# Layer 2's k-sums packed to 64 columns and moved ahead of the clip, its second reciprocal ahead of an addition, and 39 blocks in layer 3

## What is computed

```python
def _chunk_abc(q, k, v, s):
    z = jax.lax.cumlogsumexp(s, axis=2)
    g = jnp.exp(jnp.concatenate([z[:, :, :1], z[:, :, :-1]], axis=2) - z)
    p = jnp.exp(s - z)
    ...
    def step_k(hk, x):
        hk = hk * g_t[:, :, None, :] + k_t[..., None] * p_t[:, :, None, :]
        return (hk, jnp.einsum('bhk,bhkm->bhm', q_t, hk))
    ...
    pvT = jax.nn.softmax(okT, axis=-1)
    def step_v(hv, x):
        hv = hv * g_t[..., None] + p_t[..., None] * v_t[:, :, None, :]
        return (hv, jnp.einsum('bhm,bhmv->bhv', pv_t, hv))
...
s = jnp.clip(to_heads(hidden_states @ Ws, M), CLAMP_MIN, CLAMP_MAX)
o = o * jax.lax.rsqrt(jnp.mean(jnp.square(o), axis=-1, keepdims=True) + EPS) * g_norm_weight
o = o * (g * jax.nn.sigmoid(g))
return o.reshape(b, t, VALUE_DIM) @ Wo
```

```python
top_logits, top_idx = jax.lax.top_k(logits, K)
...
for e in range(E):
    h = jax.nn.silu(x @ w0[e]) * (x @ w1[e])
    out = out + cw[:, e:e + 1] * (h @ wo[e])
```

## Time and profile before

| | |
|---|---|
| median of 3 runs | 2171.97 us (2171.43 to 2173.82) |
| the profiled execution, its own time | 2193.66 us |
| its span | 2192.1 us |
| mean granted TensorE clock | 0.92 of full |
| TensorE (PE) busy | 1875.1 us, 86% |
| VectorE (DVE) busy | 1399.3 us, 64% |
| ScalarE (ACT) busy | 680.2 us, 31% |
| GpSimd (POOL) busy | 565.3 us, 26% |

### The profile page before, as it was taken

One profiled execution on the slowest core, in us unless ns is written; L12 is line 12 of the kernel. 1 busy time (PEld: TensorE's weight loads), 2 busy tenths in 40 slices (PEclk: granted clock), 3 DMA queues, 4 the chain that ended last, 5 costly groups with the idle time before them and its releaser, 6 DMA issues. The chain is left out here.

```text
span 2192.1 us, 35525 instructions
## 1 busy us (share of the span) xinstructions
PE 1875.1 (86%) x13312; PEld 1444.0 (66%) x13312; DVE 1399.3 (64%) x3037; ACT 680.2 (31%) x1205; POOL 565.3 (26%) x552
## 2 busy tenths in 40 slices
PE   5943479971999999999999997989988988989995
PEld 2341357760888888888888886455566876756663
DVE  4476355548777777777777776476656777533334
ACT  2231334441333232323333332235534323222221
POOL 0234615550021212212121211532332103401111
PEclk9975579995999999999999998999998996999998
DMA  9329224426000000000000100000001006111114
GB/s 325 122 74 296 80 82 152 151 97 199 1 1 22 1 23 12 12 23 1 23 1 23 32 1 1 1 1 2 2 1 51 27 1 240 69 37 47 47 47 134
DMA packets 100639, 134.97 MB, mean 62 GB/s; under 512 B 11616, under 2 KB 73980, under 8 KB 99968
## 3 DMA queue, kind: packets, MB, share of 16 engines
q1 hardware_dynamic: 89344, 102.16, 14.7%
q0 software_dynamic: 11136, 30.62, 3.9%
HBM read 81.94 MB, written 50.81 MB: 61 GB/s over the span
## 5 line engine op out<-in xcount | busy, mean ns | idle before, releaser
L1114 POOL TENSOR_TENSOR a_rstd<-a_ms,consts 128x8 f32<-128x8 f32 x32 | 52.4, 1638 | 590.0 <-DVE a_ms L1466 590.0
L110 PE MATMUL a_ring<-a_w_hi,l_xnT_hi 128*128 128x256 f32 x512 | 157.3, 307 | 0.0
L110 PE MATMUL a_ring<-a_w_hi,l_xnT_lo 128*128 128x256 f32 x512 | 144.2, 282 | 0.0
L110 PE MATMUL a_ring<-a_w_lo,l_xnT_hi 128*128 128x256 f32 x512 | 144.0, 281 | 0.0
L2456 POOL DMA_INDIRECT l_slots_in<-xn,f_row_of x96 | 98.5, 1026 | 97.6 <-DVE f_row_of L2750 36.6
L2983 POOL DMA_INDIRECT l_pairs_out<-f_yb,f_to_row x96 | 96.2, 1002 | 101.6 <-ACT f_yb L2958 64.2
L1219 PE MATMUL a_pab<-a_w_o,a_oT 128*128 128x256 f32 x512 | 119.2, 387 | 1.2 <-ACT a_oT L1358 1.2
L1421 DVE RECIPROCAL a_rT<-a_rT 128x256 f32<-128x256 f32 x64 | 111.4, 1742 | 0.0
L1219 PEld LDWEIGHTS a_pab<-a_w_o,a_oT 128*128 128x128 f32 x512 | 100.2, 201 | 11.6 <-ACT a_oT L1358 1.6
L1704 PE MATMUL b_ring<-b_keys,b_qm 32*128 32x128 f32 (+2 forms) x896 | 91.2, 339 | 14.9 <-DVE b_nm L1917 9.4
L1465 DVE TENSOR_REDUCE a_ms<-a_on 128x8 f32<-128x1024 f32 x32 | 39.0, 1220 | 100.9 <-ACT a_on L1378 100.9
(11 more groups left out here) (495 smaller groups left out, 5069.6 us busy)
## 6 DMA issues: line engine op xcount, KB each, us to landing
l_slots_in<-l_zeros SPq DMA_DIRECT2D x4, 3120.0 KB, 22.3
f_xb<-l_slots_in SPq DMA_DIRECT2D x11, 1040.0 KB
f_gate_up_w<-l_pairs_out SPq DMA_DIRECT2D x16, 512.0 KB, 8.7
l_slots_in<-l_zeros SPq DMA_DIRECT2D x4, 1300.0 KB, 15.4
f_xb<-l_slots_in SPq DMA_DIRECT2D x40, 130.0 KB, 2.0
f_down_w<-L_ffn_w_down_dram SPq DMA_DIRECT2D x1, 4096.0 KB
f_gate_w<-L_ffn_w_dram SPq DMA_DIRECT2D x2, 2048.0 KB, 11.1
f_up_w<-L_ffn_w_dram SPq DMA_DIRECT2D x2, 2048.0 KB, 19.8
```

The costliest lines, as they stand in the source:

```text
L110: ins = pe.matmul(out, a, b, start=start and k == 0, stop=stop and k == 2, **kw)
L1114: pool.tensor_tensor(rstd[:], ms[:], core.consts[:, C_HALF:C_HALF + 8], ALU.pow).then_inc(s["rstd_ready"], 1)
```

## The change

Four edits. The k-sums are kept as 64 columns a chunk for both heads: `chunk_sums` writes both heads' sums to the same columns and different partitions, `prefix_k` makes three instructions on 128 partitions in place of six on 64, `ok` makes two products of half the rows and half the columns for each chunk in place of one, and the memset with its semaphore goes. `prefix_k` stands ahead of the clip of s. The second half of the reciprocals stands ahead of the addition to x. Layer 3 has 39 blocks, and its slots are cleared by three transfers of 13 blocks, a row (1,040 bytes) at a time; layer 1's clearing is the same as before.

```diff
-    hk, hv = st.sb("hk", [P, 3, P]), st.sb("hv", [P, 3, DV])
+    hk, hv = st.sb("hk", [P, 3, DK]), st.sb("hv", [P, 3, DV])
...
-            pool.memset(hk[:], 0.0).then_inc(s["zeros"], 1)
...
-            pe.wait_ge(s["zeros"], 1)
...
-                        ins = pe.matmul(pc[m, c * P + DK * h:c * P + DK * h + DK], k_tok[:, k % 2, c, m],
-                                        e_tok[:, k % 2, c, m], start=True, stop=True)
+                        ins = pe.matmul(pc[m, c * DK:(c + 1) * DK], k_tok[:, k % 2, c, m], e_tok[:, k % 2, c, m],
+                                        start=True, stop=True)
...
-                pe.wait_ge(s["hk_step"], 6 * (u + 1))
+                pe.wait_ge(s["hk_step"], 3 * (u + 1))
                 for c in range(1, NCH):
-                    pe.matmul(pc[:, c * P:(c + 1) * P], hk[:, c - 1, :], qT[:, k % 2, c * P:(c + 1) * P],
-                              start=(c == 1), stop=False, skip_group_check=True)
+                    for h in range(2):
+                        m = slice(DK * h, DK * h + DK)
+                        pe.matmul(pc[m, c * P:(c + 1) * P], hk[m, c - 1, :], qT[m, k % 2, c * P:(c + 1) * P],
+                                  start=(c == 1), stop=False, skip_group_check=True)
...
-            dve.wait_ge(s["zeros"], 1)
...
-                do = Steps(dve, s["hk_step"], 6 * u, 6)
+                do = Steps(dve, s["hk_step"], 3 * u, 3)
                 for c in range(3):
-                    for h in range(2):
-                        r = slice(DK * h, DK * h + DK)
-                        new = pc[r, c * P + DK * h:c * P + DK * h + DK]
-                        if c:
-                            do(dve.tensor_tensor(hk[r, c, r], new, hk[r, c - 1, r], ALU.add))
-                        else:
-                            do(dve.tensor_copy(hk[r, c, r], new))
+                    new = pc[:, c * DK:(c + 1) * DK]
+                    if c:
+                        do(dve.tensor_tensor(hk[:, c, :], new, hk[:, c - 1, :], ALU.add))
+                    else:
+                        do(dve.tensor_copy(hk[:, c, :], new))
...
                 prefix_v(u)
+                prefix_k(u)
                 if not last:
                     project_s(n, kn)
-                prefix_k(u)
...
+                if not last:
+                    project_r(n, kn, 1)
                 if not first:
                     emit(u - 1, (k - 1) % PER)
-                if not last:
-                    project_r(n, kn, 1)
...
-        self.blocks = self.K * TILES + self.E
+        self.blocks = self.K * TILES + self.E - self.FEWER
...
 class Slots3(Slots):
+    FEWER, CLEARS = 1, 3
+
+    def clearings(self, zeros):
+        n = self.blocks // self.CLEARS
+        for k in range(self.CLEARS):
+            yield (self.xs[k * n * P:(k + 1) * n * P, :].rearrange("(n q) d -> q n d", q=P),
+                   zeros[:, 0:ROW].unsqueeze(1).to_broadcast([P, n, ROW]))
...
-                sp.wait_ge(stored[k], 16 * (NB // RING))
+                sp.wait_ge(stored[k], 16 * len(range(k, NB, RING)))
```

More of the change, by code:

```diff
@@ L1032, in layer2_abc @@
              "c_ready r_ready v_copied tanh_ready gate_ready k_turned e_turned k_tok_ready e_tok_ready "
-             "scores_ready sm_ready hk_sums hk_step ok_ready lgT_ready lg_turned hv_sums hv_step zeros logit_step ex_ready "
+             "scores_ready sm_ready hk_sums hk_step ok_ready lgT_ready lg_turned hv_sums hv_step logit_step ex_ready "
              "den_step wt_ready w_turned wT_ready am_sums am_ready ov_ready sq_ready ms_step rstd_ready "
@@ L2428, in __init__ @@
         self.router_in, self.ROUTER = st.sem("router_in"), 16 * (1 + (spec.router_bias is not None))
-        self.CLEARS = 4
     def clear(self, sp, zeros):
[L2432 to L2435, removed]
+        for rows, zero in self.clearings(zeros):
+            sp.dma_start(rows, zero).then_inc(self.cleared, 16)
     def place_pairs(self, st):
@@ L2478 @@
 class Slots1(Slots):
+    FEWER, CLEARS = 0, 4
+    def clearings(self, zeros):
+        n = self.blocks // (2 * self.CLEARS)
+        for k in range(self.CLEARS):
+            yield (self.xs[k * n * 2 * P:(k + 1) * n * 2 * P, :].rearrange("(n q i) d -> q n (i d)", q=P, i=2),
+                   zeros[:].unsqueeze(1).to_broadcast([P, n, 2 * ROW]))
     def place(self, st):
```

## The result

| | before | after |
|---|---|---|
| median of the timed runs | 2171.81 us (2171.43 to 2173.82, 4 runs) | 2144.4 us (2140.79 to 2147.38, 4 runs) |
| the profiled execution, its own time | 2193.66 us | 2147.38 us |
| its span | 2192.1 us | 2145.6 us |

The ratio is 0.9871, with a 95% interval from 0.9854 to 0.9888: 27.4 us less, a faster kernel. Forecast were 2138 us and a range from 2127 to 2157.

The account below looks back on a forecast made before the run. TensorE's queue was taken to bound layer 2's linear attention: 18.6 + 10.2 - 1.6 + 0.75 = 28.0 us, with the block 33.8, subtracted from the median 2171.97 to give 2138 us; range 2127 to 2157.

Parts of the forecast that it names:

- The k wait: Layer 2's linear attention: TensorE no longer waits for VectorE's last k-sum; 0.62 us in each of units 1 to 30, 18.6 us.
- the shape: `ok` on TensorE: twelve quarter-product records and one more change of shape cost 0.05 us more in all 32 units, 1.6 us.
- The `wT` wait: TensorE's products of `weights` no longer wait for `wT`, the reciprocal filling VectorE's idle 0.97 us; 0.33 us in 31 units, 10.2 us.
- The last unit: Without projections, TensorE waits there on VectorE, so the shorter k-sums were to give 0.75 us.
- The block: Layer 3's experts: 39 blocks run, so one period between down products goes, 5.82 us.
- Clearing and memset at nothing: Layer 3's clearing in three transfers delays nothing queued behind it, and the dropped `hk` memset was given nothing: 0 us.
- the second rival: `wT`'s input comes 0.5 us later than reckoned, so TensorE's wait there and its 10.2 us stay: 2148 us; chance 0.12.
- Quarter products take turns: `ok`: the two heads' products cannot share a bank at once; 1.42 us a group, 19 us more, 2157 us; chance 0.14.
- A new wait in the place of the old: The same claim as the second rival: TensorE still waits for `wT`, 10.2 us stay, 2148 us; chance 0.12.
- Slower: `ok`: each quarter product drains before the next, 0.28 us a record, 83 us in all, 2221 us; chance 0.04.
- Nothing seen: Both waits go but TensorE's queue is held elsewhere as long; only the block's 5.8 us stay or are lost too; chance 0.03.

Follow-up runs that it names:

- the move alone: Kernel before with only VectorE's order changed: the six 64x64 k-sum instructions ahead of the clip of s, unpacked; ratio 0.9925, 16.5 us less.
- the wide kernel: Changed kernel with k-sums back in 128 columns a chunk (six 64x64 instructions, full products, memset), still ahead of the clip; ratio 0.9865, 29.2 us below the kernel before.
- The kernel with spread statistics: Changed kernel with unpacked k-sums and the next layer norm's statistics spread over VectorE's gaps in the last unit; ratio 0.9847 to the kernel before, 32.9 us less.
- the packed k-sums with the heads outside: Changed kernel with `ok`'s two loops swapped, all three products of head 0 before those of head 1; ratio 0.9901 to the kernel before, 21.6 us less.

## Why the prediction came out as it did

**The k wait (18.6 us forecast) and the shape (-1.6 us).** The wait went, by the mechanism named: the k-sums are there a microsecond before TensorE starts on them. The two terms together were 0.62 - 0.05 = 0.57 us a unit; measured are 1.64 - 1.12 = 0.52 in the rows and 0.484 as a mean of units, where these edits stand alone. The term that was most mis-sized is the k wait. With the move alone, which leaves the shape as it was, the unit is 0.549 us shorter, not 0.62. I had taken the wait's price against unit 0, 0.99 us from the last projection to L1231. Full products further inside the stage take 1.04 without any wait (the wide kernel's rows), and that 0.05 can't be won. The shape was mis-sized too, by less. The group takes 0.80 us (I took 0.77 + 0.04), but TensorE also enters it later, 0.32 us after the last projection and not 0.23. Full products take 0.23 + 0.81 = 1.04 from there, quarters 1.12, so the shape costs 0.08 in these rows, not 0.05. By periods it is 0.041 (the changed kernel against the one with wide k-sums) or 0.066 (packing and move against the move alone).

**The `wT` wait (10.2 us forecast).** It went: 0.31 us in the rows and 0.307 as a mean of units where this edit stands alone, 0.33 forecast. What I had said of VectorE's idle 0.97 us held: the reciprocal lies in it, and the addition has no idle time left. Only unit 0 never had that wait: from its `ok` to the next one it is 21.89 us with the old order and with this edit alone.

**The last unit (0.75 us forecast).** Wrong. I read that `gated` came later by the longer k-sums and did not look at what else it needs. It reads `gr` from GpSimd. In the kernel before, GpSimd's timeline has

```profile
1332.90 1.91 POOL L1118 TENSOR_TENSOR a_gr<-a_gate,a_rstd 128x1024 f32<-128x1024 f32 x1
```

so `gr` was done at 1334.81, in the same moment as the last k-sum (VectorE's four additions ran from 1333.82 to 1334.81). TensorE's last `ok` did come 0.79 us earlier by the packing (23.45 us behind unit 30's in place of 24.24), but with the k-sums out of the way VectorE waits 0.86 us for `gr`, as the row of the changed kernel above shows, and `lgT` comes earlier only by the 0.33 us that unit 30's `wT` wait gives (29.05 us behind unit 30's `ok` in place of 29.38). The kernel with spread statistics found 1.5 us behind `gated`.

**The block (5.82 us forecast).** 6.0 us alone, 5.8 to 6.3 by the column of blocks. Clearing and memset at nothing: nothing was found against it.

**The sum.** Forecast 33.8, measured 27.4 and 28.1. From `ok` in unit 0 to `ok` in unit 30 the terms were 30 x 0.62 + 30 x 0.33 - 30 x 0.05 = 27.0 us. Measured are 0.4 (unit 0, 21.89 to 21.48) + 29 x 0.813 = 24.0. Of the missing 3.0 us, 2.5 are the mean of 29 units against 0.90 (29 x 0.087) and 0.5 are unit 0. Behind that, "end" should have become 1.0 us shorter, with unit 30's `wT` wait and the last unit. It did not: 62.5 to 64.2 in the three traces with the stage as before (the kernel before twice, and the one with 39 blocks), 64.1 to 65.2 in the three with the stage as changed (the changed kernel twice, and without the move), so 2.1 us more are missing at the means. Of them 0.65 are the last unit's term less its shape. Another 1.2 are the stretch from `lgT` to `wT`, 6.8 us at the mean of the former three and 8.0 of the latter: the granted clock, as shown above; the last 0.2 stay open. "Next" has no edited line and is 277.4 to 279.4 in the former and 280.8 to 282.3 in the latter, 3.1 at the means, of which the stretch behind it gives back 1.2 (152.3 to 151.1). These 1.9 us are clock too. Here is the stage in the kernel before and in the changed one:

```profile
1374.93:1654.32 279.39, 248.87 (x2400) 152.53 (x2401) 174.31 (x288) 112.22 (x160) 106.11 (x171) 0.96 0.01 1
1333.39:1615.69 282.30, 252.95 (x2401) 154.96 (x2402) 174.54 (x288) 112.20 (x160) 105.81 (x171) 0.94 0.01 1
```

TensorE is busy 4.1 us longer with the same records, at a lower granted clock, and the other engines are not. In all fourteen traces the stage takes 280.8 us or more at 0.94 and 279.5 or less at 0.95 and 0.96. That follows no edit: the reciprocals alone have 0.94, the packed k-sums with the heads outside 0.96, and the changed kernel itself took 282.3 us once and 280.8 once. What places the stretches at the 1.2 GHz level is open, and with one or two traces of a kernel it stays open whether the edits have a part in it. With the blocks' 6.2 by that column the sum closes: 24.0 - 1.1 - 1.9 + 6.2 = 27.2.

**The rivals.** By the time alone the second rival's 2148 us lay nearer than the forecast; it is the traces that decide. *Quarter products take turns* (1.42 us for the group): no; 0.80, and the two heads' records start in pairs. Turned about they take 1.07, and even that is less than 1.42. The Trainium skill, TensorEngine Tiling (Array Packing), Restrictions and Gotchas, says that different row tiles cannot access one PSUM bank at the same time. The runs here don't agree for products that write different partitions of the bank: products of these two row tiles start 6 ns apart, pair behind pair every 0.109 us. Its other sentence, which stands under Tiling Modes, Key Properties (and not in a section that the prediction named), that a change of mode drains the array, fits the later entry: 0.32 against 0.23 us, so 0.09 us at most, which is small. *A new wait in the place of the old*: no; the list of waits is empty, even in the kernel with wide k-sums. *Slower*: a record costs 0.067 us at the mean of the group, far from 0.15. *Nothing seen*: no.

So the forecast was right in its mechanism for both waits and the block, and 6.4 us too large. Some 3 us are the sizes of the unit's terms, the k wait's above all, priced against a unit that had it easier. About 0.7 is the last unit's term, which did not exist. The other 3 us are granted clock at the stage's end and behind it, in the traces compared. The forecast had no term for that, and it can fall either way.

## What to carry to other kernels

When a result comes late for a busy TensorE, moving its producer ahead of one instruction whose result is wanted only later can be the whole gain; the packing that came with it here was not needed, and cost TensorE 0.04 to 0.08 us a unit. Before booking a gain for a shortened chain, list every input of the next instruction, those of other engines too, and ask when each is there: `gr` was ready in the same moment as the k-sums. Before explaining a longer stage that no edit touches, lay its granted clock beside its length. And an idle time that a trace shows ahead of an instruction is slack only for what doesn't itself depend on the engine that it waits for.

## What the runs showed of the hardware

Quarter products (64*64) of two heads, in turn in the queue, run beside each other, though both write one bank, at different partitions: their records start 6 ns apart, pair behind pair every 0.109 us, so that twelve take 0.80 us. Full ones follow every 0.112 us inside the group, and six take 0.81. Twelve quarters replaced six full ones at the same time: packing saved TensorE nothing here, since the other two quarters stay empty. With three products of one head ahead of the other head's the two still overlap, only 0.275 us later (1.07 us for twelve). On VectorE a copy or an addition of 64 columns costs 0.22 to 0.25 us on 64 partitions and on 128. The same sixteen output products took 3.62 us in a stretch with a granted clock of 1.00 and 5.85 in one with 0.65, and an untouched stage was 277.3 to 282.4 us long as its clock went from 0.96 to 0.94. And some 20 us of this kernel differ between groups of runs, 17 of them in one stretch; an execution from another group would have shown as a change what is none.
